# One power instruction a turn in a four-layer graph network's dense part, first norms a turn later, ten sum buffers in the diffusion

## What is computed

```python
x = layernorm(x + gat_conv(gat_conv(x, ...), ...))
x = layernorm(x + attention(x, ...))
x = layernorm(x + layernorm(x + segment_sum(message(x[src], edge_attr), dst)) * gamma + beta)
# diffusion: h = silu(x @ W_in.T + b_in); term = out = h
for i in range(1, 7):
    term = segment_sum(term[src], dst) * inv_deg / i
    out = out + term
x = layernorm(x + out @ W_out.T + b_out)
```

## Time and profile before

| what | value |
|---|---|
| median of three runs | 3961.48 us |
| the profiled execution, its own time | 3966.26 us |
| its span in the profile | 3964.5 us |
| busy over the span | PE 3279.1, PEld 2614.1, DVE 2812.2, ACT 1892.3, POOL 2278.2 us |
| gathers of the diffusion (POOL, L595) | 600, 646.5 us |
| powers of the dense units in `diffuse` (POOL) | L720 164.6, L843 116.6, L725 113.3 us |

### The profile page before, as it was taken

One profiled execution on the slowest core, in us unless ns is written; L12 is line 12 of the kernel. 1 busy time (PEld: TensorE's weight loads), 2 busy tenths in 40 slices (PEclk: granted clock), 3 DMA queues, 4 the chain that ended last, 5 costly groups with the idle time before them and its releaser, 6 DMA issues. The chain is left out here.

```text
span 3964.5 us, 57035 instructions
## 1 busy us (share of the span) xinstructions
PE 3279.1 (83%) x14868; PEld 2614.1 (66%) x14868; DVE 2812.2 (71%) x7890; ACT 1892.3 (48%) x5401; POOL 2278.2 (57%) x2504
## 2 busy tenths in 40 slices
PE   5999927687575999468999981999999999989865
PEld 4888725576464666236777761878878787878654
DVE  5766668698685666884666660888888888888733
ACT  3777715576232111132333330565666666666555
POOL 4776500587465664133333321878878787878667
PEclk8999958899798999559999995999999999999998
DMA  5887739443474322473333339767767676767665
GB/s 148 245 246 240 227 110 362 135 131 112 138 221 134 96 88 66 121 215 97 110 111 113 114 95 305 232 209 220 233 198 234 197 236 195 237 199 230 199 206 164
DMA packets 690470, 710.73 MB, mean 179 GB/s; under 512 B 73444, under 2 KB 644190, under 8 KB 689796
## 3 DMA queue, kind: packets, MB, share of 16 engines
q1 hardware_dynamic: 592204, 484.13, 39.2%
q0 software_dynamic: 68288, 181.26, 16.0%
q10 hardware_dynamic: 29660, 41.70, 3.1%
HBM read 427.77 MB, written 296.22 MB: 183 GB/s over the span
## 5 line engine op out<-in xcount | busy, mean ns | idle before, releaser
L595 POOL DMA_INDIRECT s_i_messages<-h,table_row x600 | 646.5, 1078 | 191.6 <-issue 81.8
L2610 PE MATMUL s_i_bank<-s_i_messages,s_i_equal 128*128 128x256 f32 x1200 | 367.2, 390 | 80.4 <-DMA s_i_messages<-h,table_row 76.6
L776 PE MATMUL s_n_bank<-w,n_xt 128*128 128x256 f32 x1280 | 308.5, 385 | 20.8 <-DMA n_xt<-in_x_t 20.8
L2647 DVE SCALAR_TENSOR_TENSOR s_i_y<-s_i_bank,s_i_scale,s_i_acc 128x256 f32<-128x256 f32 x600 | 284.8, 475 | 45.0 <-PE s_i_bank L2610 26.1
L794 PE MATMUL s_n_bank<-w_out,n_ht 128*128 128x256 f32 x1280 | 309.0, 385 | 0.9 <-ACT n_ht L804 0.9
L785 PE MATMUL s_n_bank<-n_x3t,w_in 128*128 128x256 f32 x1280 | 303.5, 380 | 0.0
L816 ACT ACTIVATE n_w<-n_w,n_small 128x256 f32<-128x256 f32 x320 | 145.5, 502 | 310.3 <-POOL n_small L843 309.6
L2610 PEld LDWEIGHTS s_i_bank<-s_i_messages,s_i_equal 128*128 128x128 f32 x1200 | 220.4, 195 | 111.0 <-issue 81.7
L776 PEld LDWEIGHTS s_n_bank<-w,n_xt 128*128 128x128 f32 x1280 | 247.4, 193 | 56.2 <-DMA n_xt<-in_x_t 21.2
L794 PEld LDWEIGHTS s_n_bank<-w_out,n_ht 128*128 128x128 f32 x1280 | 247.3, 194 | 36.1 <-ACT n_ht L804 1.3
L785 PEld LDWEIGHTS s_n_bank<-n_x3t,w_in 128*128 128x128 f32 x1280 | 244.3, 191 | 33.8 <-ACT n_x3t L674 0.2
(11 more groups left out here) (426 smaller groups left out, 9424.6 us busy)
## 6 DMA issues: line engine op xcount, KB each, us to landing
h<-s_i_y SPq DMA_DIRECT2D x600, 128.0 KB
n_xt<-in_x_t SPq DMA_DIRECT2D x160, 256.0 KB
out<-n_w SPq DMA_DIRECT2D x160, 256.0 KB
s_i_equal<-eq_tab SPq DMA_DIRECT2D x600, 64.0 KB, 3.1
x<-s_x_rows SPq DMA_DIRECT2D x100, 256.0 KB
out<-s_a_hs SPq DMA_DIRECT2D x100, 128.0 KB
proj_dst<-s_a_hd SPq DMA_DIRECT2D x100, 128.0 KB
h<-s_h_rows SPq DMA_DIRECT2D x50, 256.0 KB, 3.7
```

Of the source, the lines that this page charges most:

```text
L595: return net.nc.gpsimd.indirect_dma_start(out, None, table, bass.IndirectOffsetOnAxis(index, 0))
L776: mm = self.nc.tensor.matmul(self.pr[:, g * self.D:(g + 1) * self.D], self.XT[u][:, c, g * P:(g + 1) * P], self.net.w12[:, c, :], start=c ...
L2610: nc.tensor.matmul(banks[r % 4][:, 0:D], EQ[q % NM][:], M[q % NM][:], start=True, stop=True).then_inc(summed, 1)
L2647: V.scalar_tensor_tensor(Y[q % NY][:], banks[r % 4][:, 0:D], scale[:, s, t:t + 1], acc[:, t, :], ALU.mult, ALU.add).then_inc(added, 1)
```

## The change

Three edits. The tile and the turn of the powers: `Dense` gets two tiles `powers` of 16 columns, by the turn's parity. The variances of the first norm of the unit at lag 1, of the third norm of the unit at lag 2 and of the fifth norm of the unit at lag 5 are written side by side into columns 0 to 7, and one POOL instruction of 8 columns (`powers`) raises them all and counts one semaphore, `powered`, a turn. So a unit's first two norms' powers are computed one turn later than before. ACT's `scales`, still at lag 1, move behind the squares, right in front of `last_norm`, and both wait for this turn's `powered`, as does `third_norm` on DVE. The diffusion gets ten buffers Y instead of five. SP stores before it loads in a gap. `Sources`, another class on the same base, keeps its own powers.

```diff
 class Dense(Unmet):
+    FIRST, THIRD, LAST = 1, 2, 5
...
+        self.V = self.sb("powers", [P, 16], 2)
+        self.powered = self.sem("powered")
...
+    def powers_of(self, j, u, lag):
+        i = 2 * j + u + lag
+        return self.V[i % 2], i
...
+    def scales(self, act, j, u):
+        v, i = self.powers_of(j, u, self.FIRST)
+        act.wait_ge(self.powered, i)
+        for g in range(self.G):
+            sc = self.nc.scalar.activation(self.Z[u][:, g, :], self.net.bc["gamma"][:], ACT.Identity, bias=v[:, 8 + g:9 + g],
+                                           scale=v[:, 10 + g:11 + g])
+        sc.then_inc(self.t_ready, 1)
...
     def last_norm(self, act, j, u):
-        act.wait_ge(self.dev5, j * 2 + (u + 1))
+        v, i = self.powers_of(j, u, self.LAST)
+        act.wait_ge(self.powered, i)
...
     def third_norm(self, dve, j, u):
-        dve.wait_ge(self.dev3, j * 2 + (u + 1))
+        v, i = self.powers_of(j, u, self.THIRD)
+        dve.wait_ge(self.powered, i)
...
-    def pow_5(self, gp, j, u):
-        hold(self.net, gp, self.var5_eps, j * 2 + (u + 1))
-        self.nc.gpsimd.tensor_tensor(s[:, 40:42], s[:, 38:40], self.net.neg_half[:, 0:2], ALU.pow).then_inc(self.dev5, 1)
+    def powers(self, gp, j, u):
+        v = self.V[u]
+        bases = []
+        if n := self.at(j, u, self.FIRST):
+            hold(self.net, gp, self.scales_in, n[0] * 2 + (n[1] + 1))
+            bases += [0, 4]
+        if n := self.at(j, u, self.THIRD):
+            hold(self.net, gp, self.var3_ready, n[0] * 2 + (n[1] + 1))
+            bases += [4, 6]
+        if n := self.at(j, u, self.LAST):
+            hold(self.net, gp, self.var5_eps, n[0] * 2 + (n[1] + 1))
+            bases += [6, 8]
+        if not bases:
+            return
+        b0, b1 = bases[0], bases[-1]
+        self.nc.gpsimd.tensor_tensor(v[:, 8 + b0:8 + b1], v[:, b0:b1], self.net.neg_half[:, 0:b1 - b0], ALU.pow).then_inc(self.powered, 1)
...
 (turn_act)
-        if v := self.at(j, u, 1):
-            self.scales(act, *v)
         if v := self.at(j, u, 5):
             self.square_w(act, *v)
         if v := self.at(j, u, 0):
             self.square_u(act, *v)
+        if v := self.at(j, u, 1):
+            self.scales(act, *v)
         if v := self.at(j, u, 5):
             self.last_norm(act, *v)
...
 (turn_gp)
-        if v := self.at(j, u, 5):
-            self.pow_5(gp, *v)
-        if v := self.at(j, u, 2):
-            self.pow_3(gp, *v)
-        if v := self.at(j, u, 0):
-            self.pow_1(gp, *v)
+        self.powers(gp, j, u)
...
 (diffuse)
-    NM, NY, AHEAD, CHUNK = 10, 5, 8, 10
+    NM, NY, AHEAD, CHUNK = 10, 10, 8, 10
...
             def gap():
                 i = next(n)
-                if i in at and at[i][1] < T:
-                    load_eq(at[i][0] * T + at[i][1] + AHEAD)
                 if i - 2 in at and at[i - 2][1] < T:
                     store(*at[i - 2])
                     if at[i - 2][1] == T - 1:
                         load_ends(at[i - 2][0])
+                if i in at and at[i][1] < T:
+                    load_eq(at[i][0] * T + at[i][1] + AHEAD)
```

More of the change, by code:

```diff
@@ L742, in __init__ @@
         self.HT = self.sb("ht", [P, C, G * P])
+        self.V = self.sb("powers", [P, 16], 2)
+        self.powered = self.sem("powered")
         self.xt_in = [self.sem(f"xt_loaded{u}") for u in range(2)]
         self.stored = [self.sem(f"stored{u}") for u in range(2)]
-        self.ht_ready, self.out_made, self.w_made, self.w_ready, self.var5_ready, self.var5_eps, self.dev5, self.o_ready = (
-            self.sem(n) for n in ("ht_ready", "out_made", "w_made", "w_ready", "var5_ready", "var5_eps", "dev5", "o_ready"))
+        self.ht_ready, self.out_made, self.w_made, self.w_ready, self.var5_ready, self.var5_eps, self.o_ready = (
+            self.sem(n) for n in ("ht_ready", "out_made", "w_made", "w_ready", "var5_ready", "var5_eps", "o_ready"))
         self.x3_free = self.w_made
@@ L811, in square_w @@
         sq.then_inc(self.var5_ready, 1)
+    def scales(self, act, j, u):
[5 more added lines that the diff above has]
+        sc.then_inc(self.t_ready, 1)
     def last_norm(self, act, j, u):
-        act.wait_ge(self.dev5, j * 2 + (u + 1))
+        v, i = self.powers_of(j, u, self.LAST)
+        act.wait_ge(self.powered, i)
         for g in range(self.G):
-            nm = self.nc.scalar.activation(self.W[u][:, g, :], self.W[u][:, g, :], ACT.Copy, scale=self.S[u][:, 40 + g:41 + g])
+            nm = self.nc.scalar.activation(self.W[u][:, g, :], self.W[u][:, g, :], ACT.Copy, scale=v[:, 14 + g:15 + g])
         nm.then_inc(self.o_ready, 1)
@@ L832, in add_out, with var_1 @@
         V.tensor_tensor(self.W[u][:], self.W[u][:], self.net.bc["b_out"][:].unsqueeze(1).broadcast_to([P, self.G, self.D]), ALU.add).then_inc(self.w_ready, 1)
+    def var_1(self, dve, j, u):
+        V, s = self.nc.vector, self.S[u]
+        v, i = self.powers_of(j, u, self.FIRST)
+        dve.wait_ge(self.var1_ready, j * 2 + (u + 1))
+        V.tensor_scalar(v[:, 0:2], s[:, 0:2], 1 + EPS, EPS * EPS, ALU.mult, ALU.add)
+        V.tensor_scalar(v[:, 2:4], s[:, 0:2], 1 + EPS * (1 + EPS), EPS ** 3, ALU.mult, ALU.add).then_inc(self.scales_in, 1)
@@ new lines, in var_3, with third_norm @@
+    def var_3(self, dve, ch, j, u):
+        V, s = self.nc.vector, self.S[u]
+        v, i = self.powers_of(j, u, self.THIRD)
+        hold(self.net, dve, ch.sem, ch.base + ch.k)
+        for g in range(self.G):
+            ch(V.bn_aggr(s[:, 24 + 2 * g:26 + 2 * g], s[:, 12 + 6 * g:18 + 6 * g]))
+        ch.wait()
+        V.tensor_scalar(v[:, 4:6], s[:, 25:28:2], EPS, None, ALU.add).then_inc(self.var3_ready, 1)
+        ch.close()
+    def third_norm(self, dve, j, u):
+        s = self.S[u]
+        v, i = self.powers_of(j, u, self.THIRD)
+        dve.wait_ge(self.powered, i)
+        self.past(dve, self.x3_free, j * 2 + (u - 1))
+        for g in range(self.G):
+            nm = self.nc.vector.tensor_scalar(self.X3[u][:, g, :], self.Z[u][:, g, :], s[:, 24 + 2 * g:25 + 2 * g], v[:, 12 + g:13 + g],
+                                              ALU.subtract, ALU.mult)
+        nm.then_inc(self.x3_ready, 1)
@@ L834, in var_5 @@
     def var_5(self, dve, j, u):
+        v, i = self.powers_of(j, u, self.LAST)
         dve.wait_ge(self.var5_ready, j * 2 + (u + 1))
-        self.nc.vector.tensor_scalar(self.S[u][:, 38:40], self.S[u][:, 36:38], EPS, None, ALU.add).then_inc(self.var5_eps, 1)
-    def pow_5(self, gp, j, u):
-        s = self.S[u]
-        hold(self.net, gp, self.var5_eps, j * 2 + (u + 1))
-        self.nc.gpsimd.tensor_tensor(s[:, 40:42], s[:, 38:40], self.net.neg_half[:, 0:2], ALU.pow).then_inc(self.dev5, 1)
+        self.nc.vector.tensor_scalar(v[:, 6:8], self.S[u][:, 36:38], EPS, None, ALU.add).then_inc(self.var5_eps, 1)
@@ L897, in turn_dve @@
         if third:
-            self.var_3(dve, ch, third[1])
+            self.var_3(dve, ch, *third)
         if v := self.at(j, u, 0):
```

## The result

The kernel with the change took 3922.26 us (median of four runs, 3917.63 to 3927.90) where the kernel before took 3962.85 beside it (3959.43 to 3964.93): ratio 0.9894, 95% interval 0.9880 to 0.9908. It is faster by 41 us, inside the range of the forecast, and 23 us short of its 3899. The profiled execution took 3917.63 us, with a span of 3915.9; the one before had 3964.5, so the traces show 48.6 us. They are a low run of the one and a high run of the other, and the 8 us by which they show more than the medians are scatter between runs.

What follows compares the result with a forecast made beforehand. POOL was taken to bound 124 full turns at 7.88 us, with PE next at 7.34. Powers -62, gather_out1 +3 and start -3 give -62: 3966.3 to 3904 profiled, 3899 median; range 3880 to 3938, the forecast's own 3884 to 3915.

Steps and rivals of the forecast that it cites:

- The power: On POOL in the diffusion, one eight-column power replaces three (2.39 us) and takes 1.63 us, bounds 1.32 to 2.14.
- The cover of 0.43 us for silu: In full turns silu is ready at 7.78 us, PE's next output projection comes at 8.21, so PE does not wait.
- The turns without a full load: Some 35 turns at the diffusion steps' ends with few or no gathers: zero change, 5 us either way.
- gather_out1: Its 36 dense units, set by the chain through power, scales and third variance: 6.56 us a turn, 3 us lost, bounds -2 and +12.
- Part 2: Ten buffers Y remove the 18.30 us store wait at the start: 3 us won, bounds 0 and 5; nothing in full turns.
- Part 3: SP's stores in front of loads: nothing, down to a fraction of a us won by an earlier store.
- A: Rival: POOL stays the bound of full turns at 7.66 us, gain 27 us, total 3934; chance 0.17.
- D: Rival: PE gets back only its visible idle time, 0.29 us a turn, gain 36 us, total 3926; chance 0.06.
- F: Rival: no change; gathers behind the waiting power make PE wait for messages, turn stays 7.88 us; chance 0.05.
- B: Rival: DVE, not PE, is the floor of full turns at 7.22 us, gain 82 us, total 3880; chance 0.05.
- E: Rival: the long power holds up DVE, which needs 7.52 us a turn, gain 45 us, total 3917; chance 0.03.
- C: Rival: slower; the power is held up twice to 2.65 us, POOL needs 8.14 us a turn, total 4030; chance 0.07.

Runs made afterwards that it cites:

- plain waits: Changed kernel with gather_out1's dense units as before, plus POOL's three waits before the power without counting instructions, third variance last: 3925.85 us, ratio 0.9858.

## Why the prediction was right, and where it was not

**What bounds, and what comes next.** Right. POOL bounded the 124 full turns at 7.88 (less load on it gave 7.35), and PE is next at 7.34; 7.38 was taken and 7.35 measured. That makes 124 x 0.53 = 65.7 us in place of 62.

**The power.** 1.66 us for eight columns where the straight line gave 1.63. In the diffusion it was not held up: it is released ahead of L854, as argued, and takes 1.66 to 1.67 in the whole second step. The cover of 0.43 us for silu held in full turns, since PE's transposes follow each other at PE's floor.

**The turns without a full load.** Taken as zero, 5 us either way. 18 full turns of the first step at 0.53 are 9.5 us of its 10.6, which leaves 1 for the start; all six steps together gained 60.7, and 60.7 - 65.7 - 1 is 6 us lost in the short turns. In these the power is on a chain and not a load, and each hand-over to POOL costs the 0.24 us more that the forecast did not have. That it is this which costs the 6 us is argued from the same row. What the runs show is that the shorter turn by itself does not cost it: the kernel without the fifth power has the same full turn of 7.35, and its five steps gained 61.4 us, of which 106 full turns at 0.53 make 56; it gained in the short turns. The plain waits took 0.10 us off each hand-over and 0.9 us off the five steps, too little to tell.

**gather_out1.** The failed step: a loss of 3 us, measured 12, the end of its bound. The chain was the right one (the first), but its term "three hand-overs 0.12" was mis-sized: the 0.04 us each was read from ACT, which starts 0.04 us behind POOL, and taken for the hand-over from DVE to POOL too. In the mean of the 35 turns the three took 0.29 us (variance to power), 0.04 (power to scales) and 0.09 (scales to scale and shift), 0.41 together, and the power 1.69 and not 1.63, since eight were held up. The rest of the chain came as forecast: scale and shift to the variance's end 3.72 for 3.73, the scales 1.09 for 1.08. The sum is 6.92, the turn measured. The forecast also took 6.47 for the turn of before, from the row of L823; the row of L688 has 6.60, by which the forecast chain of 6.56 would have lost nothing. With this stage moved back its turn is 6.58.

**Part 2.** "Gone with ten buffers" was right about the wait of 18.30 us at the start, but what was next in line was not one message that was 5 us late, but SP itself, 28.9 us in issuing two DMAs: about 1 us won, not 3, by what the first step leaves. And **"In full turns the add waits for no store: nothing"** was wrong, by most of the gain. It was read off the trace of before, where it is true. The change lets the adds run earlier against PE and the turn be shorter, but the last norm waits for the one power and ends where it did against PE. So SP stands at the output's store as before, and behind it the stores of Y, which the adds now need sooner. That this place in SP's list is the cause is shown, by the move of the one store; how much each part takes from the room is read from single turns of the traces. The forecast listed who waits for the power on ACT and on DVE, and left out that a third queue waits for ACT. The sum came out near because the change carries the cure with it, and this was luck, for the forecast gave the buffers 3 us at the start alone: without the ten buffers the forecast of 3899 would have been for a kernel that gains nothing.

**Part 3.** Nothing, as forecast, beside ten buffers; beside five it is worth about half of the wait.

**The sum.** Forecast -62 + 3 - 3 = -62; the traces show -65.7 (full turns) + 6 (short turns) - 1 (start) + 12 (gather_out1) = -48.7. The medians show 41, for after's profiled execution is 4.6 below its median and that of before lay above its own. After's four runs fall at 3917.6, 3917.8, 3926.7 and 3927.9; what divides them stays open, since one trace shows one run.

**The rivals.** A (POOL stays the bound, 7.66) is refuted by POOL's idle time, D (7.59) and F by the turn of 7.35. B (DVE bounds, 7.22) is refuted too: in full turns PE has no idle time, and with the dense pipeline full its turn of four tiles goes under 7.34 in none of the kernels, whatever is taken from POOL. The total of 3922 alone would not have told them apart, for it lies between those of D (3926) and E (3917); the turn does. The Trainium skill (Trainium Kernel Development and Optimization, Performance Expectations) has weight loads' busy share as the good measure. It is 79% over the stretch (1035.46 of 1315 us), which would leave a fifth in reserve, but 88% in full turns (123.31 of 140 us), so not half of that fifth lies in the steps' ends; of the 12% left in full turns no run here found any. C's mechanism, a held-up power, is seen, but in gather_out1, at up to 1.92 instead of 1.66, and not in the full turns of the diffusion's second step. E did not come: L854 started beside the power and took 0.69 us.

## What to carry to other kernels

When a step is moved later, follow it through every queue that waits for its result, and then ask what stands behind that wait in the same queue: a DMA queue that serves two pipelines passes a delay from the one to the other. Two edits that remove two bounds of the same turn must be costed together, since each alone may show nothing. And a merge of instructions pays where their engine is full; where it has idle time, the same merge lengthens the chain by the wait for the last operand.

## What the runs showed of the hardware

- A hand-over from DVE to a waiting POOL took longer than one from POOL to ACT: 0.28 us from the third variance to the power at 3007.05, and once 0.61 in gather_out1, where ACT began 0.03 us behind the power (860.41 to 860.44). The waits themselves are part of it: with plain waits, the third variance's last, it was 0.18 us.
- A VectorE instruction with two operands in SBUF (L854, 3008.04) took its usual 0.69 us inside a power of 1.67 us. The Trainium skill (SBUF — State Buffer, SBUF: two separate sides) has such a pair lock each other out for the whole instruction; this row does not agree with it, while the power that took 1.92 us (851.15) started 0.03 us behind a dot product with two operands in SBUF (851.12). All eight powers of gather_out1 that took 1.76 us or more began inside such a dot product of 0.42 us, and the later in it the shorter: 1.92 us at 0.03 behind its start, 1.87 at 0.08, 1.76 at 0.18. So the hold-up is seen in one direction. No run tried the two by themselves.
- Issuing one DMA from SP, 0.45 us in the usual turn, took 16.57 and 12.32 us at the start of the diffusion. A load that stands behind such an issue in SP's list is late by all of it.
